# Constant-row lookups padded from 96 to 128 rows, the variance sum folded before its matmul, and t's lookups one u unit later

## The reference

```
h = ln(ln(x, pw_g[pathway], pw_b[pathway]), cp_g[kind], cp_b[kind])
t = ln(x, tm_g[kind], tm_b[kind])
s = ln(x, ms_g[scale], ms_b[scale])
m, n, r = x + mlp_ln(memory | noise | resource state of the batch row)
cat = concat(w0*h, w1*t, w2*m, w3*n, w4*r, w5*s)      # w = softmax(aw), 3072 features
x1 = x + ln(silu(cat @ W1 + b1) @ W2 + b2, g, be)
y = clip(((x1 * style) @ weight.T) * dcoef + bias, -256, 256)
out = x1 + y
```

## Time and profile before

| what | value |
|---|---|
| median of three runs | 1159.75 us |
| the profiled execution | 1159.39 us |
| its span, first to last instruction | 1157.6 us |
| TensorE (PE) busy | 1137.3 us, 98% |
| VectorE (DVE) busy | 933.6 us, 81% |
| ScalarE (ACT) busy | 676.0 us, 58% |
| GpSimd (POOL) busy | 238.0 us, 21% |
| granted TensorE clock | 0.999 of full |

### The profile page before, as it was taken

One profiled execution on the slowest core, in us unless ns is written; L12 is line 12 of the kernel. 1 busy time (PEld: TensorE's weight loads), 2 busy tenths in 40 slices (PEclk: granted clock), 3 DMA queues, 4 the chain that ended last, 5 costly groups with the idle time before them and its releaser, 6 DMA issues.

```text
span 1157.6 us, 14923 instructions
## 1 busy us (share of the span) xinstructions
PE 1137.3 (98%) x5036; PEld 925.2 (80%) x5036; DVE 933.6 (81%) x1752; ACT 676.0 (58%) x970; POOL 238.0 (21%) x268
## 2 busy tenths in 40 slices
PE   5999999999999999999999999999999999999998
PEld 4667888888888888888888888888888888888886
DVE  6898978879698787969879697896969879697836
ACT  3647475574746557375574746557375574747553
POOL 3441222213122211212212122220212212022000
PEclk9999999999999999999999999999999999999999
DMA  9953262333425233352423425333352424425001
GB/s 327 352 180 72 84 178 82 123 76 119 125 82 164 75 110 102 91 162 82 130 69 128 117 82 164 88 112 88 101 152 82 137 65 134 111 82 158 13 1 73
DMA packets 115372, 135.23 MB, mean 117 GB/s; under 512 B 69824, under 2 KB 70208, under 8 KB 115200
## 3 DMA queue, kind: packets, MB, share of 16 engines
q1 hardware_dynamic: 99872, 83.32, 25.6%
q0 software_dynamic: 14336, 50.34, 13.7%
q10 hardware_dynamic: 1088, 0.62, 0.2%
HBM read 101.74 MB, written 16.78 MB: 102 GB/s over the span
## 4 chain that ended last, share of the span: by engine, by line
PE 86%; DVE 9%; ACT 2%; issue 1%; DMA 1%; POOL 1%; SPq 0%; DVEq 0%; POOLq 0%; ACTq 0%
PE pre L1243 13%; PE pre L1247 13%; PE pre L1250 13%; PE uy L1301 5%; PE uy L1302 5%; PE uy L1304 5%; PE uy L1314 4%; PE uy L1317 4%; PE pre L1283 4%; PE uy L1315 4%; PE pre L1282 4%; PE pre L1281 4%; PE turn L1222 3%; PE pre L1264 1%; DMA ug<-x_in 1%
## 5 line engine op out<-in xcount | busy, mean ns | idle before, releaser
L435 POOL TENSOR_TENSOR ra<-vea,half 128x1 f32<-128x1 f32 x64 | 48.3, 754 | 374.9 <-DVE vea L825 374.9
L594 ACT ACTIVATE hi_a<-xT,style 128x512 fp32r<-128x512 f32 x60 | 43.5, 725 | 133.2 <-DVE xT L925 133.2
L1301 PE MATMUL uy<-hi_c,w_hi_w 128*128 128x512 f32 x256 | 101.4, 396 | 0.0
L602 ACT ACTIVATE ug<-uy,cols,dcoef 128x512 f32<-128x512 f32 x56 | 43.5, 776 | 98.5 <-PE uy L1317 98.5
L1304 PE MATMUL uy<-lo_c,w_hi_w 128*128 128x512 f32 x256 | 100.3, 392 | 0.3 <-DVE lo_c L880 0.2
L1281 PE MATMUL pre<-hi_b,w_hi_x 128*128 128x512 f32 x256 | 99.9, 390 | 0.6 <-DVE w_lo_x L1054 0.6
L1302 PE MATMUL uy<-hi_c,w_lo_w 128*128 128x512 f32 x256 | 100.0, 391 | 0.0
L1283 PE MATMUL pre<-lo_b,w_hi_x 128*128 128x512 f32 x256 | 99.7, 389 | 0.0
L1282 PE MATMUL pre<-hi_b,w_lo_x 128*128 128x512 f32 x256 | 99.6, 389 | 0.0
L857 DVE TENSOR_TENSOR lo_a<-tmp_a,hi_a 128x512 fp32r<-128x512 f32 x64 | 44.2, 690 | 66.3 <-ACT hi_a L521 66.2
L417 POOL DMA_INDIRECT gb<-pw_table,pw_ids x63 | 71.0, 1127 | 125.3 <-DMA whole_b<-gb 108.8
(11 more groups left out here) (241 smaller groups left out, 2934.1 us busy)
## 6 DMA issues: line engine op xcount, KB each, us to landing
xT<-x_turned SPq DMA_DIRECT2D x64, 256.0 KB, 2.8
out_turned<-xT SPq DMA_DIRECT2D x64, 256.0 KB, 2.0
xt<-x_in SPq DMA_DIRECT2D x62, 256.0 KB, 2.6
sel_in<-sel_ids SPq DMA_DIRECT2D x16, 192.0 KB, 2.8
raw_s<-int_w SPq DMA_DIRECT2D x2, 512.0 KB, 11.0
raw_h<-int_w SPq DMA_DIRECT2D x1, 1024.0 KB, 23.3
early_hi_w<-mlp_w SPq DMA_DIRECT2D x1, 1024.0 KB, 19.0
raw_w<-mlp_w SPq DMA_DIRECT2D x1, 1024.0 KB, 21.3
```

What stands on the lines that cost most here:

```text
L1301: pe.matmul(bank, w_hi["w2"][:, c, cut], hi["c"][:, c, :], start=c == 0, stop=False)
```

## The change

1. `rows` and the three tables get 128 partitions; rows 96 to 127 are zero. POOL clears a 32x1024 piece of staging memory at its start, ACT copies it once into `rows`, later once into `tab_b`; the t and s tables get theirs by being copied over 128 rows. PE waits once for each (`quad_set`). All lookups and offsets then run over 128 rows.
2. After the last square, DVE adds the upper 64 partitions of `sq0` to the lower 64 (`fold_sum`). The high part of the folded sum (64 partitions) goes to the lower half of `sum_r` and the rest to its upper half, so that one matmul over 128 rows gives the variance.
3. The inverse root is cut in two; `low_h(i, 3)`, which stood behind it (ahead of it for i = 1), stands between its halves.
4. In the loop, t's first three lookups for the next group stand after `unit_u` 1, 2 and 3; ACT's `split_t` 0 and 1 move likewise; `low_hid(i, 3)` comes ahead of `pick_rows`.
5. POOL issues two `gather_gb` and one `gather_gc` ahead of `rstd_x(f)` (f is the next group's first tile).

```diff
@@ buffers
-        rows = sb("rows", [TROWS, GROUP], F32R)
-        tab = {n: sb(f"tab_{n}", [TROWS, D], F32R) for n in "tsb"}
+        rows = sb("rows", [P, GROUP], F32R)
+        tab = {n: sb(f"tab_{n}", [P, D], F32R) for n in "tsb"}
@@ POOL, start
             pool.wait_ge(half_set, 1)
+            nc.gpsimd.memset(tmp["b"][TROWS:P, 0:2, :], 0.0).then_inc(quad_zero, 1)
+            pool.wait_ge(quad_zero, 1)
@@ POOL, loop
                 if more:
-                    rstd_x(f)
                     gather_gb(f)
                     gather_gb(f + 1)
                     gather_gc(f)
+                    rstd_x(f)
                     gather_gb(f + 2)
@@ ACT, split_sum
-                act.wait_ge(sq_added, 3 * i + 3)
-                nc.scalar.activation(sum_r[:, 0, :], sq0[:], ACT.Copy).then_inc(sum_hi, 1)
+                act.wait_ge(sq_folded, i + 1)
+                nc.scalar.activation(sum_r[0:HALF, 0, :], sq0[0:HALF, :], ACT.Copy).then_inc(sum_hi, 1)
@@ ACT, start
             nc.scalar.activation(vmat[:], tmp["a"][:, 0, 0:2], ACT.Copy).then_inc(vmat_ready, 1)
+            act.wait_ge(quad_zero, 1)
+            nc.scalar.activation(rows[TROWS:P, :], tab_raw["t"][TROWS:P, :], ACT.Copy).then_inc(quad_set, 1)
...
             table_high("s")
+            nc.scalar.activation(tab["b"][TROWS:P, :], tab_raw["s"][TROWS:P, :], ACT.Copy).then_inc(quad_set, 1)
@@ ACT, loop
                 u_out(i, 0)
                 if more:
-                    split_t(n, 0)
                     gate(n * TPG + 2)
                 u_out(i, 1)
                 if more:
+                    split_t(n, 0)
                     part_halves(n * TPG + 2)
+                u_out(i, 2)
+                if more:
                     split_t(n, 1)
-                u_out(i, 2)
@@ DVE
+            def fold_sum(i):
+                dve.wait_ge(sq_added, 3 * i + 3)
+                nc.vector.tensor_tensor(sq0[0:HALF, :], sq0[0:HALF, :], sq0[HALF:P, :], ALU.add).then_inc(sq_folded, 1)
+                dve.wait_ge(sq_folded, i + 1)
+
             def low_sum(i):
                 dve.wait_ge(sum_hi, i + 1)
-                nc.vector.tensor_tensor(sum_r[:, 1, :], sq0[:], sum_r[:, 0, :].bitcast(F32), ALU.subtract).then_inc(sum_lo, 1)
+                nc.vector.tensor_tensor(sum_r[HALF:P, 0, :], sq0[0:HALF, :], sum_r[0:HALF, 0, :].bitcast(F32), ALU.subtract).then_inc(sum_lo, 1)
@@ DVE, loop
                 add_square(i - 1, 3)
+                fold_sum(i - 1)
                 make_t(i, 3)
...
-                if i == 1:
-                    low_h(i, 3)
-                find_root(i - 1)
-                if i > 1:
-                    low_h(i, 3)
+                find_root(i - 1, lambda: low_h(i, 3))
...
+                low_hid(i, 3)
                 if more:
                     pick_rows(n)
-                low_hid(i, 3)
-                if more:
                     low_rows(n)
@@ PE
-                pe.matmul(bank, vmat[:, 0:1].to_broadcast([P, P]), sum_r[:, 0, :], start=True, stop=False)
-                pe.matmul(bank, vmat[:, 0:1].to_broadcast([P, P]), sum_r[:, 1, :], start=False, stop=True).then_inc(turn_filled, 1)
+                pe.matmul(bank, vmat[:, 0:1].to_broadcast([P, P]), sum_r[:, 0, :], start=True, stop=True).then_inc(turn_filled, 1)
...
                 for o in range(C):
                     unit_u(i, o)
-                    if more and o < 3:
-                        gain("t", n, o)
+                    if more and o > 0:
+                        gain("t", n, o - 1)
```

More of the change, by code:

```diff
@@ L25 @@
 TROWS = 3 * QUAD
+HALF = P // 2
 EPS = 1e-5
@@ L118, in build @@
         b2_in, row_raw = ug[:, 2, :], ug[:, 3, 0:3 * C * QUAD]
-        tab_raw = {"t": tmp["b"][0:TROWS, 0, :], "s": tmp["b"][0:TROWS, 1, :]}
+        tab_raw = {"t": tmp["b"][:, 0, :], "s": tmp["b"][:, 1, :]}
         aff_raw, gc_stage = early_hi["l1"][:, 0:2, :], {1: early_hi["l1"][:, 2, :], 2: early_hi["l1"][:, 3, :]}
@@ L151, in build @@
         aw_max, aw_exp, aw_ready = sem("aw_max"), sem("aw_exp"), sem("aw_ready")
-        half_set, stat_set, vmat_set, vmat_ready = sem("half_set"), sem("stat_set"), sem("vmat_set"), sem("vmat_ready")
+        half_set, vmat_set, vmat_ready = sem("half_set"), sem("vmat_set"), sem("vmat_ready")
+        quad_zero, quad_set = sem("quad_zero"), sem("quad_set")
         tab_hi, tab_ready = {n: sem(f"tab_hi_{n}") for n in "ts"}, {n: sem(f"tab_ready_{n}") for n in "tsb"}
@@ L160, in build @@
             sem(n) for n in ("batch_copied", "bias_ready", "low_copied", "dsum_copied"))
-        style_ready, l1_sq, dco_in, dco_ready = (
-            sem(n) for n in ("style_ready", "l1_sq", "dco_in", "dco_ready"))
+        style_ready, l1_sq, dco_in = (sem(n) for n in ("style_ready", "l1_sq", "dco_in"))
         wr_scaled, wx_sum, w2_mean, b2_ready = (
@@ L176, in build @@
         v_done, rows_hi, rows_ready, b_used = sem("v_done"), sem("rows_hi"), sem("rows_ready"), sem("b_used")
-        sq_added, sum_hi, sum_lo, var_read, root_step, root_ready = (
-            sem(n) for n in ("sq_added", "sum_hi", "sum_lo", "var_read", "root_step", "root_ready"))
+        sq_added, sq_folded, sum_hi, sum_lo, var_read, root_ready = (
+            sem(n) for n in ("sq_added", "sq_folded", "sum_hi", "sum_lo", "var_read", "root_ready"))
         t_raw, t_hi, t_lo, t_used = sem("t_raw"), sem("t_hi"), sem("t_lo"), sem("t_used")
@@ L335, in _ @@
                 load_xT(0, c)
-            put("tab_s", tab_raw["s"], tab_src[1])
+            put("tab_s", tab_raw["s"][0:TROWS, :], tab_src[1])
             put_part("s", 5, 0)
@@ L555, in split_rows @@
                 after(act, b_used, i)
-                nc.scalar.activation(rows[:], sel_in[:].bitcast(F32), ACT.Copy).then_inc(rows_hi, 1)
+                nc.scalar.activation(rows[0:TROWS, :], sel_in[:].bitcast(F32), ACT.Copy).then_inc(rows_hi, 1)
             def hidden(i, o):
@@ L607, in _ @@
             put("aw", soft[:, 0, :], aw.rearrange("(a k) -> a k", a=1).to_broadcast([P, 6]))
-            put("tab_t", tab_raw["t"], tab_src[0])
+            put("tab_t", tab_raw["t"][0:TROWS, :], tab_src[0])
             act.dma_start(raw_w["t"][:, 0, :], int_w1[D:D + P, :]).then_inc(w_loaded["t"][0], 16)
@@ L895, in inverse_root @@
[L895 to L911, removed]
+                nc.vector.tensor_tensor(sum_r[HALF:P, 0, :], sq0[0:HALF, :], sum_r[0:HALF, 0, :].bitcast(F32), ALU.subtract).then_inc(sum_lo, 1)
+            def begin_root(v, y, h):
+                link(nc.vector.tensor_scalar(y.bitcast(I32), v.bitcast(I32), -0.5, MAGIC, ALU.mult, ALU.add))
+                link(nc.vector.tensor_tensor(h, y, y, ALU.mult))
+                link(nc.vector.tensor_tensor(h, v, h, ALU.mult))
+                link(nc.vector.scalar_tensor_tensor(out=h, in0=h, scalar=-10.0 / 3.0, in1=h, op0=ALU.add, op1=ALU.mult))
@@ new lines, in end_root, with find_root @@
+            def end_root(v, y, h):
+                link(nc.vector.scalar_tensor_tensor(out=y, in0=h, scalar=5.0, in1=y, op0=ALU.add, op1=ALU.mult))
+                link(nc.vector.tensor_tensor(h, y, y, ALU.mult))
+                link(nc.vector.scalar_tensor_tensor(out=h, in0=h, scalar=-27.0 / 1024.0, in1=v, op0=ALU.mult, op1=ALU.mult))
+                return nc.vector.scalar_tensor_tensor(out=y, in0=h, scalar=9.0 / 16.0, in1=y, op0=ALU.add, op1=ALU.mult)
+            def find_root(i, between):
@@ L913, in find_root @@
                 dve.wait_ge(var_read, i + 1)
-                inverse_root(sq[2], root[:], sq0[:], chain, root_ready)
+                begin_root(sq[2], root[:], sq0[:])
+                between()
+                end_root(sq[2], root[:], sq0[:]).then_inc(root_ready, 1)
             def make_x1(i, c):
@@ L1128, in _ @@
                     dve.wait_ge(dco_in, 1)
-                    inverse_root(small[:, 1], dcoef[:], small[:, 0], link, dco_ready)
-                    dve.wait_ge(dco_ready, 1)
+                    begin_root(small[:, 1], dcoef[:], small[:, 0])
+                    link(end_root(small[:, 1], dcoef[:], small[:, 0]))
                     low_h(i, 2)
@@ L1221, in gain @@
                     pe.wait_ge(tab_ready[which], 1)
+                    pe.wait_ge(quad_set, 1)
                 pe.matmul(bank, tab[which][:, c * P:(c + 1) * P], rows[:], start=True, stop=True).then_inc(turn_filled, 1)
@@ L1268, in first_offsets @@
                 pe.wait_ge(tab_ready["b"], 1)
+                pe.wait_ge(quad_set, 2)
                 for o in range(C):
```

## The result

| | before | after |
|---|---|---|
| median | 1159.4 us (4 runs, 1158.22 to 1159.75) | 1191.57 us (4 runs, 1186.97 to 1193.97) |
| ratio, 95% interval | | 1.0275 [1.0241, 1.0308] |
| profiled execution | 1159.39 us | 1193.97 us |
| TensorE busy | 98% | 96% |
| one group (mean of groups 2 to 14) | 69.21 us | 71.73 us |

The changed kernel is 2.75% slower, where 1152.3 us and at most 1156.6 were forecast. A group's time here is the distance from the first `unit_t` matmul of group 2 to that of group 15, over 13.

What follows compares the result with a forecast made beforehand. PE, busy 98%, was taken as the bound: matmul count times pitch. From 1159.39 us, 3.4 for the variance matmul and 3.9 for padding came off, other parts costing nothing: 1152.1, as median 1152.3, range 1151.0 to 1156.6.

Steps and rivals of the forecast that it cites:

- POOL's order: Three gathers ahead of `rstd_x(f)` fit in POOL's 6.90 us of idle time: no cost, up to 1 us as bound.
- Case C: Padding's excess only partly goes, or small new waits take 1 to 3 us back: 1153.5 to 1155 us; chance 0.12.
- Padding: Lookups and offsets over 128 rows on PE: removes long pitches, 0 to 3.9 us in all; upper end taken.
- Rival B: Padding lookups and offsets does nothing; only the variance matmul and late first lookup count: median 1156.0 us; chance 0.31.
- One variance matmul less: On PE, 15 times a pitch of 0.227 us saved, 3.4 us, plus 0.1 us of excess.
- The fold: One more DVE pass, 0.7 us, 0.73 with its wait, 15 times; hidden from PE, 0.5 us to spare.
- rival D: DVE's fold across partitions costs far more than a pass, PE waits behind the variance: slower, 1164.2 at 1.8 us; chance 0.03.
- t's lookups later: On PE, t's lookups one unit later get 1.8 us of slack: no cost, some 0.02 us of excess a group gone.
- `low_h(3)` in the root: On DVE, fills a chained wait between the root's halves: no cost; if group 1's cover fails, under 1 us once.
- the set-up: POOL's memset and ACT's copies at the start lie in idle time or delay chunks needed later: no cost.
- The sum: Whole kernel: 1159.39 - 3.4 - 3.9 = 1152.1 us, given as a median of 1152.3.
- It is wrong if PE waits in each group: Sign against the forecast: PE waiting every group, first of all at the lookup behind the variance.

Runs made afterwards that it cites:

- p1_rows96: `e1_pool_back` with lookups and offsets read over 96 of the 128 rows again: 1155.55 us, ratio 0.9963.
- p2_no_fold: `e1_pool_back` without the fold, with two variance matmuls as before: 1156.05 us, ratio 0.9970.
- e1_pool_back: The changed kernel with POOL's old order, `rstd_x(f)` ahead of the three gathers: 1153.06 us, ratio 0.9946.
- e4_gathers_wait: The changed kernel, gathers still ahead of `rstd_x(f)`, but POOL issues them only once the fourth transpose has landed: 1152.3 us, ratio 0.9937.
- b1_fold_later: `e1_pool_back` with the fold moved behind `make_t(3)` and `make_s(0)` on DVE: 1152.74 us, ratio 0.9942.
- d1_one_ahead: The changed kernel with one gather ahead of `rstd_x(f)` and the other two behind it: 1153.45 us, ratio 0.9950.
- d2_two_ahead: The changed kernel with two gathers ahead of `rstd_x(f)` and the third behind it: 1154.06 us, ratio 0.9952.

## Why the prediction was wrong

**POOL's order** is the step that failed: "No cost, up to 1 us as a bound". I had seen the two facts that it takes, that the gathers move beside a transpose, and that ACT waits 2.08 us for that transpose already. Then I made two mistakes. First, I gave "if it lands later" no size. The trace of before had one, in the stretch where the gathers ran then (columns as above):

```profile
606.00:614.00 8.00, 8.00 (x37) 6.60 (x36) 7.69 (x13) 2.08 (x3) 4.80 (x5) 1.00 0.63 187
```

1.25 MB at 187 GB/s are 7 us, so that 3.1 us of landing could become 10 if the transpose was served behind them. I took POOL's own slack (three issues of 1.4 us fit in 6.90 us of idle time, which was right, `rstd_x` was not late) for the slack of the transfers. Second, I followed the late landing to the wrong reader. I looked at `low_h(3)` on DVE and at the x1 chain, which is worth 3.1 of the 39.1 us. The first reader is ACT: `join_halves(3)` and `split_h(3)`, whose `lo_c` is the operand of the very first h matmul. That path has 24.05 - 15.4 - 2.05 - 3.1 = 3.5 us of slack, and the landing took 5.6 more. Case C had "the transpose behind the gathers" with 1 to 3 us in all; the mechanism stood there with a price ten times too low, since a wait that comes in each of 14 groups was priced as if it came once or twice. The "slower" side got 0.03, all of it for the fold.

The Trainium skill has a sentence that bears on this: "DMA: Bandwidth & Descriptors", section "Issuing engines are not separate DMA queues", says that DMAs started by the scalar, sync or gpsimd engine run on the same 16 DMA engines and interleave, whichever engine started them. The traces agree: the transpose comes from SP and the gathers from POOL, and 3.1 us became 8.7. In the prediction I wrote that on SP nothing is moved, and stopped there.

**Padding** was right, and its upper end was the right one: forecast 0.25 us a group less, measured 0.23 (`p1_rows96`); for the whole kernel forecast 3.9 us, measured 3.3 by the trace and 2.5 by the medians. (The three excesses as printed add up to 0.29 us and not 0.28, which changes nothing.) Rival B, that it does nothing, is out. The Trainium skill, "TensorE: Matmul & The Clock Gate", Part 2, says that the row count doesn't matter for the time of a weight load. The traces agree as far as the load's own row goes, 0.188 us with 96 rows and with 128. For the pitch it does not hold: 68.95 us a group with 96 rows and 68.72 with 128, all else the same. The matmul's own row differs too, 0.395 us on average with 96 rows and 0.389 with 128. In the prediction I took 0.40 us twice for agreement, but both were rows of uneven forms.

**One variance matmul less** was right: 0.25 us a group measured (`p2_no_fold`), 0.227 and 0.01 forecast.

**The fold** was priced at 0.7 us and took 0.69, so rival D is out. It is hidden in groups 2 to 14, but not in group 1, which I had not looked at for this step: 1.1 us once. And "hidden" held only while PE set the pace; in the kernel that was run, it was not.

**t's lookups later, `low_h(3)` in the root, the set-up**: no cost in `e1_pool_back`, as forecast; PE waits nowhere in its groups 2 to 14.

**The sum** without the failed step: forecast 68.7 us a group and 1152.3 us. `e1_pool_back` has 68.72 and 1153.06 (group 1, with its 1.1 us of the fold, was not in the sum), `e4_gathers_wait` 1152.3, `b1_fold_later` 1152.74. So the terms of TensorE were good to under 1 us, and one term that was written down as nothing was 38.5. "It is wrong if PE waits in each group" came true, at the h units and not, as I had it, at the lookup behind the variance.

All three beat both the kernel before and the changed one, as do `d1_one_ahead`, `d2_two_ahead`, `p1_rows96` and `p2_no_fold`; `b1_fold_later`, with the narrowest interval of the three, is 0.58% [0.45, 0.72] faster than before.

## What to carry to other kernels

When an edit moves a DMA's issue, price its bytes: what else is in flight then, how late can that land (bytes over the rate that the trace shows, as a lower bound, since here the two kinds of transfer slowed each other), and who is its first reader, on every engine. Slack of the engine that issues says nothing about slack of the transfers. A cost hidden behind a bound engine is hidden only as long as that engine stays the bound: once another chain sets the pace, each delay on it counts in every round, and savings on the old bound turn into waiting.

## What the runs showed of the hardware that I had not expected

- A transpose by DMA of 128x1024 two-byte elements lands 3.1 us after its issue by itself, 4.7 us with some 0.75 MB of gathers ahead, 5.5 with 1 MB, 8.7 with 1.25 MB (medians). The last 256 KB, issued 0.15 us ahead of the transpose, cost the most. The gathers and the transpose together take some 9 us in the changed kernel, from the first packet of the one to the last of either; apart they take about 4.8 and 1.4 us. Why the growth is so uneven stays open.
- fp32r matmuls of 128 x 128 by 512 columns run at 0.2266 us a pitch; a matmul whose weight tile has 96 rows or repeats one column makes its own pitch and the next few longer, by 0.02 to 0.03 us in all for a lone one. Its own row is longer by 0.006 to 0.008 us (0.395 and 0.397 against 0.389), and the row of its weight load is not (0.188 us).
- In 4 of 13 groups, PE had stood idle for 1.9 to 3.1 us ahead of the h units and the granted clock then was at half for 8 to 14 of their first matmuls. In the other nine it stayed at full, with idle times of 2.44 and 2.61 us among them (the latter in the group shown first).
- A DVE addition whose inputs lie on partitions 0 to 63 and 64 to 127 takes 0.69 us, the same as a pass in one place.
